# Propagation rounds of a four-layer graph network: ScalarE, not SyncE, begins the store of each batch's values

## What is computed

```python
h = x
for _ in range(16):
    h_neighbors = jax.ops.segment_sum(norm * h[row], col, num_segments=N)
    h = (1.0 - ALPHA) * h_neighbors + ALPHA * x
```

## Time and profile before

| what | value |
|---|---|
| median of 3 runs (lowest to highest) | 13499.98 us (13473.8 to 13504.35) |
| profiled execution: its span | 13552.9 us |
| ScalarE busy | 3099.7 us (23%) |
| GpSimd busy | 9980.6 us (74%) |
| VectorE busy | 6176.6 us (46%) |

### The profile page before, as it was taken

The page is one execution under the profiler, slowest core; times in us unless marked ns, Lnnn a source line. Parts: engine busy times, 40 slices in busy tenths (PEclk is TensorE's granted clock), DMA queues, the critical chain, the costliest instruction groups (busy, mean ns, idle before and its releaser), DMA issues. The chain is left out here.

```text
span 13552.9 us, 124135 instructions
## 1 busy us (share of the span) xinstructions
PE 6161.5 (45%) x16702; PEld 3564.8 (26%) x16702; DVE 6176.6 (46%) x21955; ACT 3099.7 (23%) x11470; POOL 9980.6 (74%) x10210
## 2 busy tenths in 40 slices
PE   6422105873002555555555555555555555544000
PEld 4322103542001322223323332323322322233000
DVE  4344455596343444444444444444444444444533
ACT  5300133394000222222222222222222222233000
POOL 7677777676777777777777777777777777777777
PEclk8655557886555777777777777777777777755555
DMA  5433353374223333333333333333333333344245
GB/s 150 120 99 100 109 145 97 92 216 142 76 75 89 117 112 112 118 112 112 116 112 112 118 112 112 116 112 112 117 112 112 116 113 112 116 132 129 73 116 140
DMA packets 855833, 1558.86 MB, mean 115 GB/s; under 512 B 321698, under 2 KB 378674, under 8 KB 855666
## 3 DMA queue, kind: packets, MB, share of 16 engines
q1 hardware_dynamic: 523217, 1053.28, 22.9%
q0 software_dynamic: 332448, 504.04, 16.3%
HBM read 954.90 MB, written 602.08 MB: 115 GB/s over the span
## 5 line engine op out<-in xcount | busy, mean ns | idle before, releaser
L340 POOL DMA_INDIRECT r_g<-y_t,idx_s x6272 | 6051.0, 965 | 2128.7 <-issue 2115.0
L349 DVE SCALAR_TENSOR_TENSOR r_S<-r_S,scan_s,r_g 128x96 f32<-128x96 f32 x6272 | 2020.3, 322 | 4670.1 <-DMA r_g<-y_t,idx_s 3968.8
L1421 PE MATMUL r_pu<-r_S,ident 128*128 128x384 f32 x2940 | 1883.7, 787 | 3127.9 <-DVE F L351 3127.9
L1443 ACT ACTIVATE H<-r_pu,k_e 128x96 f32 (+1 forms) x5880 | 1443.3, 356 | 6059.3 <-PE r_pu L1421 6059.3
L351 DVE SCALAR_TENSOR_TENSOR F<-r_g,scan_s,F 128x96 f32<-128x96 f32 x6272 | 1967.6, 314 | 0.0
L1421 PEld LDWEIGHTS r_pu<-r_S,ident 128*128 128x128 f32 x2940 | 737.9, 276 | 3947.0 <-DVE F L351 3583.5
L1415 PE MATMUL r_pu<-H,ident 128*128 (+1 forms) x2940 | 1633.0, 646 | 101.5 <-DMA r_c<-c_t 101.5
L340 POOL DMA_INDIRECT n_ag<-agg_t,idx_s x1176 | 1227.2, 1044 | 395.8 <-issue 368.4
L1416 PE MATMUL r_pu<-r_c,ident 128*128 128x384 f32 x2940 | 1441.4, 578 | 0.0
L1415 PEld LDWEIGHTS r_pu<-H,ident 128*128 128x128 f32 x2940 | 824.4, 281 | 816.9 <-issue 683.4
L1416 PEld LDWEIGHTS r_pu<-r_c,ident 128*128 128x128 f32 x2940 | 712.4, 242 | 599.2 <-issue 383.0
(11 more groups left out here) (233 smaller groups left out, 7251.4 us busy)
## 6 DMA issues: line engine op xcount, KB each, us to landing
y_t<-H SPq DMA_DIRECT2D x784, 384.0 KB, 2.4
r_c<-c_t SPq DMA_DIRECT2D x735, 384.0 KB
r_g<-y_t,idx_s POOLq DMA_INDIRECT x6272
n_x<-x_t SPq DMA_DIRECT2D x147, 384.0 KB, 4.5
kv_t<-n_kvq SPq DMA_DIRECT2D x49, 768.0 KB, 3.7
agg_t<-e_S SPq DMA_DIRECT2D x98, 384.0 KB, 2.6
x_t<-n_x SPq DMA_DIRECT2D x98, 384.0 KB, 2.4
y_t<-n_y SPq DMA_DIRECT2D x98, 384.0 KB
```

Source lines behind the costliest of these rows:

```text
L340: G.indirect_dma_start(out=to(j), out_offset=None, in_=table, in_offset=bass.IndirectOffsetOnAxis(ap=idx_s[:, h, j:j + 1], axis=0)).then_i ...
L349: own.add(V.scalar_tensor_tensor(out=S[:, h % slots, j, 0:w], in0=before, scalar=scan_s[:, h, j, 0:1], in1=g[:, j, 0:w], op0=ALU.mult, op1 ...
L1421: last = T.matmul(pu[h % 2][g][:], ident[:], S[:, h % 2, 4 * g:4 * g + 4, :], start=False, stop=True)
L1443: last = A.activation(v[:, j, :], pu[h % 2][j // 4][:, j % 4, :], ACT.Copy, scale=k[:, j:j + 1])
```

## The change

The `store` stage leaves SyncE. ScalarE, at the end of `value`, waits for its own last activation (`s_s`), raises a turn semaphore that nobody waits for, and issues the same 384 KB DMA with the same completion semaphore `s_st`. SyncE keeps the loads of `r_c` and the 48 KB store of `r_zs`.

```diff
@@ SyncE
-                        def store(b, n, h):
-                            after(sp, s_s, r * NB + b + 1)
-                            sp.sem_inc(s_turn_s)
-                            sp.dma_start(rows_of(to, VALUES, b), cols(H, b)).then_inc(s_st, 16)
                         after(sp, s_up, r * NB)
                         sp.sem_inc(s_turn_s)
-                        skewed(sp, (1, store), (-1, load))
+                        skewed(sp, (-1, load))
                         after(sp, s_z, r + 1)
                         sp.dma_start(to[VALUES + AUX:VALUES + AUX + P, :], zs[:]).then_inc(s_zo, 16)
@@ ScalarE
                             last.then_inc(s_s, 1)
+                            after(act, s_s, r * NB + b + 1)
+                            act.sem_inc(s_turn_a)
+                            A.dma_start(rows_of(y_t[1 - odd], VALUES, b), v).then_inc(s_st, 16)
```

More of the change, by code:

```diff
@@ L265, in program @@
         Z = sb("Z", [P, WZ])
-        s_turn_v, s_turn_p, s_turn_s = (nc.alloc_semaphore(name=f"{e}_turns") for e in ("vector", "pool", "sync"))
+        s_turn_v, s_turn_p, s_turn_s, s_turn_a = (nc.alloc_semaphore(name=f"{e}_turns")
+                                                  for e in ("vector", "pool", "sync", "scalar"))
         s_w = sem("weights_loaded")
```

## The result

The changed kernel takes 13537.15 us (median of 10 runs, 13520.88 to 13542.08) against 13498.21 us (13473.8 to 13509.83, 10 runs) for the kernel before: a ratio of 1.0028, with a 95% interval of 1.0019 to 1.0037. It is slower by about 39 us. The forecast was 13505 us and "no change", in a range from 13477 to 13537 us. The time came out at the upper edge of that range, 32 us over the forecast, and the 39 us are more than the 27 us that the prediction itself took as the least change that can be told.

The account below looks back on a forecast made before the run. GpSimd's row gathers and 14 round-end waits were taken as the bound. Ends inside the body +5.9 us, entry or turns -0.9, last end -0.2: together +5 us, so 13505 us, range 13477 to 13537.

Parts of the forecast that it names:

- GpSimd never waits inside a round: Inside a round GpSimd issues a gather each 1.25 us without standing still; moving the stores there sums to 0.
- The last chain of a round decides, 14 times: At 14 inner round ends GpSimd waits 14.8 us for the last gather, sum, addition, values and stores.
- ScalarE's wait for its own last activation equals SyncE's 0.10 us: At a round's end, ScalarE's store issue follows its last activation by 0.10 us; +0.25 us per end kept for the range.
- Alone that gives -0.26 us: At an end inside the loop's body, the earlier `r_zs` store leaves `H` as releaser, gaining 0.26 us without collision.
- I take +1.1 us inside the body: At 7 ends inside the loop's body, the next loads share DMA engines with the `H` store, delaying it 1.1 us.
- At the turn ... the remaining 0.47 us doubles: Where the loop turns, the store has 0.5 us alone, then sharing adds 0.47 us, against a gain of 0.6.
- cover of 3 us: At a round's end, the next round's first slots are copied about 3 us before GpSimd starts, covering delays of ScalarE.
- ScalarE becomes late: Rival: a DMA issue holds ScalarE until landing, delaying slots; a 5 us hold costs 28 us, 13528 us; chance 0.03.
- The bytes stay the same ... so I expect no difference: Gathers in the rounds keep their 960 ns mean though the load moves 3 us forward; 76 us hang on this.
- I carry 5 us over to it: The round-end terms' sum of +5 us is added unscaled to the median of the runs, giving 13505 us.
- own sign of being wrong: Wrong if GpSimd pauses inside a round, mean gather moves 5 ns or more, or round ends move over 1.9 us each.
- both loads go ahead of the store: Rival: at every round end the store waits 2.5 us for two loads; +35 us, 13535 us; chance 0.09.

Follow-up runs that it names:

- Run 1: Changed kernel with the last of each round's 49 stores back on SyncE, ahead of `r_zs` and the next loads: 13474.25 us against 13478.59, ratio 0.9997 to the kernel before.
- Run 2: Changed kernel with SyncE holding the next round's `r_c` loads until all 49 stores landed: 13499.28 us against 13478.59, ratio 1.0013 to the kernel before.
- Run 7: Kernel before, all on SyncE, with each load ahead of the store and `r_zs` ahead of the last `H` store: 13456.87 us against 13457.5, ratio 1.0000.
- run 8: Changed kernel with only the next round's batch 1 load held until the stores landed, batch 0's going at once: 13495.55 us against 13457.5 for the kernel before, ratio 1.0029.
- Run 5: Kernel before, with ScalarE only waiting for its last activation of each round, issuing no DMA: 13457.44 us against 13457.5, ratio 1.0000.
- run 9: Changed kernel with 24 tiny copies on ScalarE ahead of its loop, shifting the loop's code 24 places: 13493.77 us against 13473.41 for the kernel before, ratio 1.0013.
- run 12: Kernel before plus ScalarE's wait for its last activation and 21 tiny copies in each round's code, no DMA on ScalarE: 13469.91 us against 13459.52, ratio 1.0008.
- run 10: Kernel before plus ScalarE's wait for its last activation and 21 tiny copies ahead of its loop, no DMA on ScalarE: 13471.21 us against 13473.41, ratio 0.9997.
- run 3: Kernel before with 12 tiny copies added to ScalarE's code in each written-out round, loop body 526 instructions instead of 502: 13484.94 us against 13478.59, ratio 1.0003.
- Run 4: Kernel before, all stores on SyncE, with the `r_c` load issued ahead of the store in each tick: 13470.62 us against 13478.59, ratio 0.9994.

## Why the prediction was right or wrong

**GpSimd never waits inside a round: right.** Outside the round ends its gaps stay at 0.30 us, and the 19 us of slack hid ScalarE's 735 issues. Run 1, with 720 of them, is even with the kernel before.

**The last chain of a round decides, 14 times: right.** The release moved from the `r_zs` store to the store of `H`, as forecast, at 8 of 14 ends.

**"ScalarE's wait for its own last activation equals SyncE's 0.10 us": right,** 0.11 us at the end shown. Of the rows of SyncE's loads and ScalarE's stores that overlap in time, some ten of each, none is longer than 0.37 us, so the row of 0.7 us that the prediction gives for issues so close did not show.

**"Alone that gives -0.26 us": the sign right, the size not.** Run 2 has 3.47 us from the store's issue to GpSimd where the kernel before has 3.58, so 0.1 us. Run 7 could not see any gain.

**"I take +1.1 us inside the body": mis-sized, the collision cost 2.1 us.** The mechanism, a load that follows `r_zs` to its earlier place and meets the store, is shown by run 2, and that one load does it by run 8. The ends were forecast at 15.6 us; they came to 16.6. The error lies in the price of a whole load, 1.26 us, worked out from two loads back to back at 81% of the engines. A load that starts with nothing ahead of it is slower: 99 of its 128 packets took the 2 us from 9371.0 to 9373.0. The cited rule of "DMA: Bandwidth & Descriptors" in the Trainium skill (rings served in turn, a packet each) fits if its packet is taken as it describes it, a run of some 9 to 17 descriptors: a store has 8 rows per engine, so each engine would serve the load's share whole before it turns. No run here varies the number of rows to test that.

**"At the turn ... the remaining 0.47 us doubles": the step that failed, in two ways.** I forecast -0.13 us at such an end. First, nothing doubles: the store, issued 0.47 us ahead, has all its data moved 2.5 to 2.6 us after the last activation, and the loads come behind it (2.3 to 2.6 us at the turns of run 2, where no load was out). Second, and this is the loss, the store isn't what GpSimd waits for. ScalarE's slots came 6.6 us after the last activation, at 8864.18. Their cover of 3 us was read at an end inside the body and taken for the turn too, where ScalarE already stood idle for 0.82 us without a releaser before the change.

The rival "ScalarE becomes late" put the place right and the cause wrong: it asked whether a DMA holds ScalarE until it lands. What it takes is two things.

First, the branch. Before, ScalarE goes through it while its 8 activations still run, and some 2 us of the stall are hidden; the wait on the last activation puts the branch behind them. Run 5 shows this without any DMA.

Second, a further stall between `idx_s` and `scan_s`, which depends on where the loop stands in the code (run 9). The Trainium skill ("Advanced Engine Details and Errata", ISA Cache) gives ScalarE two lines of 256 instructions. By that rule a top that ends one line and begins the next needs two loads, if the turn finds neither line there. The effect of the shift agrees with it. That the listed body grew over 512, from 502 to 543, explains neither stall: the first comes at 502 as well (run 5), and run 12 gave no second stall at 543, nor did run 10 at 502 or, without the wait, run 3 at 526. The exact places, with the unlisted instructions, were not reproduced. So it is shown that the second stall is one of the code's place, and not shown which lines are involved. That it needs a DMA on ScalarE as well is not excluded: the changed kernel, run 2 and run 8, which show it, all issue the last store of a round on ScalarE.

**"The bytes stay the same ... so I expect no difference" for the gathers: right.** The changed kernel's 956 ns against 960 looked like a gain of some 20 us; runs 3 and 4 have 954 each.

**"I carry 5 us over to it": 39 us measured.** The forecast's 5 us lack 8 ends of 1 us and 6 of some 4 us, which makes 32 us. By the prediction's own sign of being wrong, round ends that move by more than 1.9 us each, it fails: the six moved by 3.7 us, all 14 by 2.6 in the mean. Its chance for a loss of over 0.2% was 0.16. That the time still lies at the edge of the range is luck: the bound came from the rival "both loads go ahead of the store", whose 13535 us fit the time closely, but run 8 shows that the first load alone makes the collision, and the larger part of the loss, the six turns, is not in that rival at all.

No version beat both kernels by what can be measured. Run 4 is nearest (0.9994, interval up to 1.0003), and run 7, its extension, is at 1.0000.

## What to carry to other kernels

When a store leaves a queue, look at what stood behind it there. Here it was the next round's loads, which moved forward into the one transfer that the whole kernel waits for; a wait of one line on them took that back. A DMA that an engine issues on its own result needs a wait, and a wait ahead of a branch lets the engine reach the branch only when its queue is empty, so that the stall there is no longer hidden. Leave the DMA of the last batch to another engine, as run 1 did at no cost. And read the slack of a wait at each kind of round end, the one at the loop's turn too: the cover read inside the body did not hold there.

## What was unexpected in the hardware

- Of two 384 KB transfers on different queues, the one issued 0.18 us (the load) or 0.47 us (the store) ahead moved nearly all its data first. With the load ahead, GpSimd was released 1.96 us later than before the change. Issued 0.07 us apart, they once ran side by side (run 8).
- ScalarE stood idle for 3.0 to 3.7 us after its last instruction ahead of a backward branch, when it reached the branch with nothing queued (runs 5, 9, 12), and for 0.83 us with its 8 activations ahead (run 1).
- 24 unused instructions ahead of a loop moved the kernel's ratio from 1.0028 to 1.0013.
- A single 8192-byte packet of the `instruction` queue, passing while the last stores of a round landed, went with a release 0.74 us later (run 12 against run 5).
- In a hardware loop with an address from a register, one DMA of ScalarE is three instructions, two of which (42 and 29 ns) the listing of the program does not have.
